# Six gathers at a time: GpSimd waits for landings while it fetches the source terms of a graph layer

## The reference

```python
# layer 1, cut to what matters
xn = layernorm(x)
x = x + gat_and_gcn(xn, edge_index, edge_weight, ...)   # needs, for every edge e, terms[src[e]] (4 numbers)
      + linear_attention_block(xn, ...)                 # keys/values, then queries and a 256-1024-256 MLP
```

## Time and profile before

| | |
|---|---|
| time, median of 2 runs | 11597.03 us (11595.1 to 11598.96) |
| span of the profiled execution | 13601.5 us |
| instructions | 139964 |
| PE, PEld busy | 8472.8 us (62%), 5970.4 us (44%) |
| DVE, ACT busy | 4716.6 us (35%), 1395.1 us (10%) |
| POOL busy | 5341.4 us (39%) |
| mean granted TensorE clock | 0.760 |

### The profile page before, as it was taken

How to read it: one execution, slowest core, us unless ns; L and a number is a source line. 1 busy time by engine, 2 the same in 40 slices (tenths; PEclk the granted TensorE clock), 3 DMA queues, 4 the chain that set the end, 5 groups by cost and what they waited for, 6 DMA issues and landing times. The chain is left out here.

```text
span 13601.5 us, 139964 instructions
## 1 busy us (share of the span) xinstructions
PE 8472.8 (62%) x31420; PEld 5970.4 (44%) x31421; DVE 4716.6 (35%) x15039; ACT 1395.1 (10%) x3054; POOL 5341.4 (39%) x6235
## 2 busy tenths in 40 slices
PE   3666666688889741511112888600777777778798
PEld 2333444455567531211112666400455555544687
DVE  4333333321132310200001555322666666654300
ACT  0000000013312200000000222100000000000121
POOL 2666666610000046077765000143666666630100
PEclk7677777788879876855556888755998888975699
DMA  5333322221010330100000000003666666652101
GB/s 170 89 88 88 86 85 83 82 77 41 22 54 21 128 85 11 38 6 5 6 4 7 17 17 17 21 20 111 176 178 184 184 191 193 196 159 81 52 18 52
DMA packets 568905, 1068.90 MB, mean 79 GB/s; under 512 B 161007, under 2 KB 295402, under 8 KB 568155
## 3 DMA queue, kind: packets, MB, share of 16 engines
q0 software_dynamic: 283600, 692.27, 18.9%
q1 hardware_dynamic: 252316, 328.10, 8.0%
q10 hardware_dynamic: 32927, 47.77, 1.0%
HBM read 894.49 MB, written 175.61 MB: 79 GB/s over the span
## 5 line engine op out<-in xcount | busy, mean ns | idle before, releaser
L1863 POOL DMA_INDIRECT agg_rows<-node_rows,agg_stage x1660 | 1618.1, 975 | 906.1 <-issue 490.2
L618 POOL DMA_INDIRECT agg_rows<-xn_rows,agg_stage x1660 | 1585.1, 955 | 688.5 <-issue 439.6
L674 PE MATMUL agg_ps_sum<-agg_rows,agg_sel_w 128*128 128x257 f32 x3320 | 1336.1, 540 | 715.0 <-DVE agg_sel L639 433.0
L1913 PE MATMUL agg_ps_g<-agg_rows,agg_sel_w 128*128 128x256 f32 x3320 | 1172.3, 438 | 516.9 <-issue 285.4
L2167 POOL DMA_INDIRECT mix_lots<-src_terms,mix_idx_stage x1196 | 1138.3, 952 | 415.0 <-issue 368.8
L638 DVE TENSOR_SCALAR agg_sel_w<-iota,dst_item,w_item 128x128 f32<-128x128 f32 x1660 | 688.9, 415 | 1561.4 <-DMA agg_rows<-xn_rows,agg_stage 1416.2
L674 PEld LDWEIGHTS agg_ps_sum<-agg_rows,agg_sel_w 128*128 128x128 f32 x3320 | 673.7, 252 | 1069.3 <-issue 996.6
L1914 PE MATMUL agg_ps_a<-agg_att,agg_sel 128*128 128x260 f32 x3320 | 1105.2, 417 | 0.9 <-DVE agg_att L1894 0.5
L1894 DVE TENSOR_TENSOR agg_att<-agg_rows,ee_item 128x256 f32<-128x256 f32 x1660 | 707.8, 426 | 937.5 <-DMA agg_rows<-node_rows,agg_stage 869.5
L1913 PEld LDWEIGHTS agg_ps_g<-agg_rows,agg_sel_w 128*128 128x128 f32 x3320 | 644.9, 211 | 868.0 <-issue 526.9
L2430 PE MATMUL mix_ps_h<-mix_x1t,mix_w 128*128 128x256 f32 x1600 | 431.6, 430 | 531.3 <-issue 416.5
(11 more groups left out here) (463 smaller groups left out, 13035.1 us busy)
## 6 DMA issues: line engine op xcount, KB each, us to landing
xn_turned<-norm_xt SPq DMA_DIRECT2D x200, 256.0 KB
agg_rows<-xn_rows,agg_stage POOLq DMA_INDIRECT x1660
agg_rows<-node_rows,agg_stage POOLq DMA_INDIRECT x1660
xn_rows<-norm_xn SPq DMA_DIRECT2D x100, 256.0 KB
ctx_xt<-xn_turned SPq DMA_DIRECT2D x100, 256.0 KB
mix_xt<-xn_turned SPq DMA_DIRECT2D x100, 256.0 KB
ffn_xt<-xn_turned SPq DMA_DIRECT2D x100, 256.0 KB
node_rows<-tab_rows POOLq DMA_DIRECT2D x50, 512.0 KB
```

The lines of the kernel that those rows point to most:

```text
L618: pool.indirect_dma_start(rows[:, u, 0:C], None, g.xn_rows, bass.IndirectOffsetOnAxis(stage[:, u:u + 1], 0)).then_inc(landed[u], 16)
L674: pe.matmul(ps_sum[:, to], sel_w[:, u, :], rows[:, u, :], start=False, stop=False, skip_group_check=True)
L1863: pool.indirect_dma_start(rows[:, u, :], None, g.node_rows, bass.IndirectOffsetOnAxis(stage[:, u:u + 1], 0)).then_inc(landed[u], 16)
L1913: pe.matmul(ps_g[:, to], sel_w[:, u, :], rows[:, u, 0:C], start=False, stop=False, skip_group_check=True)
```

## The change

Inside the loop over the 23 gathers of a lot, GpSimd now stops after gathers 6, 12 and 18. It waits until all gathers of this lot so far have landed (16 counts each), and a `sem_inc` carries this wait. Nothing waits for the semaphore `issued`. The last five gathers of a lot are followed by no such wait. There are three waits in each of 68 lots: 48 in `context1` and 156 in `mix1`, 204 in all. The gathers, their data and all other instructions stay.

```diff
 LOT = 23
+BREATH = 6
 FETCH_LOTS = -(-PER // LOT)
 CTX_LOTS = 16
...
                 for i in range(LOT):
                     pool.indirect_dma_start(self.lots[:, u, i, :], None, g.src_terms,
                                             bass.IndirectOffsetOnAxis(self.stage[:, u, i:i + 1], 0)).then_inc(self.landed[u], 16)
+                    if i % BREATH == BREATH - 1:
+                        pool.wait_ge(self.landed[u], 16 * LOT * k + 16 * (i + 1))
+                        pool.sem_inc(self.issued, 1)
                 if not (first and u == 0):
                     v = 1 - u
                     pool.wait_ge(self.landed[v], 16 * LOT * (k if u == 0 else k + 1))
```

## The result

The changed kernel takes 12,003.5 us (two runs, 11,998.6 and 12,008.5) where the kernel before takes 11,597.0: 406.5 us more, a ratio of 1.035 with a 95% interval of 1.032 to 1.038. It is slower, as forecast, by 3.5% and not by 2.5%, and it lies 3.5 us above the upper end of the stated range.

What follows compares the result with a forecast made beforehand. Without the profiler, GpSimd's fetch was taken to bound context1 and mix1. 204 waits at 1.73 us add 353 us, less 65 hidden: 11,597 + 288 = about 11,890 us, 2.5% slower, range 11,600 to 12,000.

Steps and rivals of the forecast that it cites:

- The account of the 2004 us: Profiled span over plain time: 1664 us from context1 and mix1, 470 from the aggregations, leaving 11,468 against 11,597 us.
- The fetch's excess over the groups: Without the profiler, GpSimd's fetch outlasts the groups by some 90 us in context1 and some 130 in mix1.
- The stall: Beside the fetch in context1 and mix1, TensorE's matmuls are answered 34.5 us late; taken as almost wholly the recording's doing.
- A: Stall in context1 and mix1 is real and the trains cure it: 1311 us gained, about 10,290 us; chance 0.15.
- C: Stall is real and the waits don't cure it: 300 us more, 11,900 us; chance 0.05.
- The wait's price: GpSimd stands until the train's last gather has landed: 1.73 us per wait, 204 waits, 353 us (253 to 414).
- The upper bound: Per wait in the fetch, the whole 0.79 us start of a gather on idle GpSimd comes on top: 2.03 us.
- The cover: Groups of mix1 that outlast the fetch hide part of the waits' 270 us there: 65 us, half of 129.
- the 129 us that the account left over: Gap between 11,468 us and the 11,597 us of the runs, possibly groups of mix1 that outlast the fetch.
- 470 us: Aggregations' excess in the profile: 331 batches at 0.65 and 0.77 us over unhindered ones of 7.00 and 7.07.
- The prediction's own range for its case: Whole kernel if the fetch binds and the stall is the recording's: 124 to 414 us more, 11,720 to 12,010 us.
- Rival B: The 0.30 us between gathers and the stall are the recording's; no measurable difference, about 11,720 us; chance 0.14.

Runs made afterwards that it cites:

- half kernel: Kernel before with only every second gather of a lot issued (816 of 1564), no added waits: 11,418.5 us, 178.7 less than before.
- clean trace: Profile of the kernel before, run again unchanged: 11,594.2 us against 11,592.4, ratio 1.000, span of the profiled execution 11,591.3 us.

## Why the prediction was right and wrong

**What binds, right.** The account of the 2004 us put the two stages at 2190 us without the profiler. They take 2203. Both are bound by GpSimd's fetch: runs with more waits, with fewer gaps and with half of the gathers show it from three sides. The fetch's excess over the groups was put at some 90 and 130 us. The half kernel shows 522 - 446 = 76 and 1681 - 1578 = 103.

**The stall, half right.** "If the stall were real" was rightly denied, and with it rivals A and C. What the prediction took from it about the recording went too far: it expected recording to stall TensorE in this kernel as a rule ("since recording stalls TensorE in it"). Two more profiles of the same kernel show no stall, so its being "almost wholly the recording's doing" holds for one execution at most. That the block of the trace records held TensorE back was only argued, and no run shows it. What stretched that one execution stays open.

**The wait's price, the term that was mis-sized.** The step "I add the difference: 1.54 + 0.49 - 0.30 = 1.73 us per wait" measured 1.94 in the trace and 1.99 in the time. The gather starts some 0.8 us behind the landing: 2.4 us from issue to landing less 0.95 us of issue are 1.45, and 2.24 - 1.45 leaves 0.79, the idle time of a gather behind its index copy. The 2.4 is rounded, so this split is good to 0.05 us. If attention's gathers land as late, its copy in the earlier trace rows starts within 0.1 us of the landing (1.54 - 1.45), and too much was deducted from the 0.79: the prediction added 0.79 - 0.30 = 0.49 to the 1.54 and then took the 0.30 off a second time. The upper bound, 2.03, was nearly the value. This makes 204 x 0.21 = 43 us of the missing 118.

**The cover, the step that failed.** "I take half, 65 us" rested on the 129 us that the account left over, read as groups that may outlast the fetch; that it was half of them had no row behind it. They were no groups. The clean trace takes (2612.0 - 260.9)/331 = 7.10 and (10097.7 - 7673.7)/331 = 7.32 us per batch of the aggregations, not the 7.00 and 7.07 of single unhindered batches. So 470 us had been taken off where the time from the first copy to the last, 2533.2 and 2593.8 us against 2351.1 and 2424.0, shows 182 + 170 = 352 in excess, and 118 of the 129 us were this. With the 3854 - 2203 = 1651 us of the two stages these 352 make 2003 of the 2010 us by which the stretched span exceeds the clean one: the stretch lies in these four stages. mix1's groups end 103 us before its fetch (1681 - 1578), nothing is covered, and the full price is paid. Without the 65 us and with the measured wait the sum is 396 us.

**The rest.** 396 against 406.5 leaves 10 us, of which the two stages hold 3 (399); the place of the others no run shows. The 204 gaps are where they were forecast, at 2.24 us on average, near the upper end of the 1.8 to 2.3, though single ones last up to 4 us, and gathers last 0.95 us as before. The prediction's own range for its case, 11,720 to 12,010, holds the measured time; the stated one stopped at 12,000 and left that tail out. Rival B (the 0.30 us between gathers are the recording's) is out: they stand unchanged in recorded executions whose spans, 11,591.3 and 11,589.1 us, are no longer than the 11,597.0 us measured without the profiler.

## What to carry to other kernels

Where one engine only issues small DMAs and its line of work is the longest of the stage, every pause that lets its queue run dry is paid in full: here 1.94 us, landing and restart together, and the number of pauses times that gives the added time within 3% from 48 to 476 of them. The same pauses are free where another line of work is longer (11,417.0 us with them, 11,418.5 without). A wait for completion cost nothing here when it asked for the batch before the one just issued. Before reading a trace for what stalls whom, hold its span against the time measured without the profiler; if they differ by 17%, take a second profile, or at least don't spend the remainder of an account on a term of the sum.

## What the runs showed of the hardware

A gather of 128 rows of 16 bytes takes GpSimd 0.95 us to issue, 0.30 us of lead-in behind another gather, and lands 2.4 us (2.2 to 3.5 in the changed kernel's trace) after its start. On an idle GpSimd the lead-in is 0.79 us. With trains of three the median to landing is 2.3 us, and single gathers took up to 6.0. One recorded execution was 17% longer than the timed ones, unevenly: in it mix1 took 3021 us for 1681, and the aggregations 7 to 8% more. Eight of TensorE's matmuls were recorded within 4.53 us there (3.60 in the clean trace) and yet answered 34.5 us late, so such a trace looks like contention and names no culprit. Whether the profiler did this isn't shown.
